# Row maxima as full-array products, and TensorE's step in another order, in a one-core transformer block

## The reference

```python
h = _L0_tok_ref(x, W, b, pos)                       # patches @ W.T + b + pos, 32 x 1024 x 64
q = h @ Wq.T + bq; k = h @ Wk.T + bk; v = h @ Wv.T + bv
scores = einsum('bid,bjd->bij', q, k) / 8           # 1024 x 1024 for each image
prob = softmax(scores)                              # rows with q[0] == 0 or k[0] == 0 become 0
h = layernorm(h + (prob @ v) @ Wo.T + bo)
idx = argmax(softmax(h @ gate_w + gate_b))          # expert of each token
pos = (cumsum(one_hot) * one_hot).sum(-1) - 1       # its place in the expert's list, kept if < C
y = relu(buf @ w1 + b1) @ w2 + b2                   # by expert, 64 -> 256 -> 64
h = layernorm(h + nan_to_num(y[idx, pos] * prb * kept))
```

## Time and profile before

| what | value |
|---|---|
| median of 3 runs | 1159.21 us (1153.78 to 1161.12) |
| profiled execution, span | 1163.1 us |
| TensorE busy | 1029.4 us, 89% |
| VectorE busy | 902.7 us, 78% |
| GpSimd busy | 692.6 us, 60% |
| ScalarE busy | 728.6 us, 63% |

### The profile page before, as it was taken

How to read it: one execution, slowest core, us unless ns; L and a number is a source line. 1 busy time by engine, 2 the same in 40 slices (tenths; PEclk the granted TensorE clock), 3 DMA queues, 4 the chain that set the end, 5 groups by cost and what they waited for, 6 DMA issues and landing times.

```text
span 1163.1 us, 18855 instructions
## 1 busy us (share of the span) xinstructions
PE 1029.4 (89%) x5534; PEld 582.2 (50%) x5534; DVE 902.7 (78%) x1847; ACT 728.6 (63%) x1142; POOL 692.6 (60%) x689
## 2 busy tenths in 40 slices
PE   4899999999999999999999999999999999736640
PEld 2455555555555555555555555555555555423320
DVE  5557787789898988889888988898988887654542
ACT  2255455667777777677777776776777667535540
POOL 0014445447676676667767666766666767765665
PEclk8699999999999999999999999999999999866775
DMA  5324335444444443535344443443453613034300
GB/s 129 93 69 106 96 89 141 111 104 111 115 122 115 109 121 96 148 87 150 95 125 120 114 104 106 124 119 101 106 137 79 154 37 92 20 96 121 98 18 10
DMA packets 76732, 118.93 MB, mean 102 GB/s; under 512 B 16652, under 2 KB 52959, under 8 KB 76630
## 3 DMA queue, kind: packets, MB, share of 16 engines
q1 hardware_dynamic: 59798, 100.61, 34.6%
q0 software_dynamic: 16832, 17.11, 4.6%
...
## 4 chain that ended last, share of the span: by engine, by line
PE 55%; DVE 24%; issue 10%; ACT 4%; SPq 2%; another core or an unknown queue 1%; POOL 1%; DMA 1%; POOLq 0%; DVEq 0%; ACTq 0%
PE p_u L575 15%; DVE mx L979 8%; PE p_st L559 8%; PE p_st L562 7%; PE p_sm L545 5%; PE p_misc L508 4%; PE p_misc L531 4%; PE p_misc L638 3%; PE p_misc L654 2%; PE p_misc L590 2%; ACT xh L754 2%; DVE ld L1045 1%; POOL out L1355 1%; DVE tt L1006 1%
## 5 line engine op out<-in xcount | busy, mean ns | idle before, releaser
L1343 POOL DMA_INDIRECT slots<-rows,idx x256 | 261.7, 1022 | 220.5 <-issue 151.4
L771 ACT ACTIVATE pT<-p_st 128x1024 f32<-128x1024 f32 x256 | 262.2, 1024 | 171.9 <-PE p_st L562 131.4
L979 DVE TENSOR_REDUCE mx<-p_sm 128x1 f32<-128x1024 f32 x252 | 307.3, 1220 | 80.1 <-PE p_sm L545 69.5
L1355 POOL DMA_INDIRECT out<-b_o,b_ix x270 | 286.9, 1063 | 111.9 <-issue 73.4
L575 PE MATMUL p_u<-pT,vv 128*64 128x512 f32 x1024 | 263.8, 615 | 0.0
L559 PE MATMUL p_st<-mQ,sK 128*128 128x512 f32 x512 | 184.2, 441 | 5.5 <-ACT pT L771 3.6
L562 PE MATMUL p_st<-mR,sR 72*128 72x512 f32 x512 | 161.8, 397 | 0.0
L545 PE MATMUL p_sm<-sK,mQ 64*128 64x512 f32 x252 | 130.7, 519 | 6.9 <-DVE mx L979 3.4
L559 PEld LDWEIGHTS p_st<-mQ,sK 128*128 128x128 f32 x512 | 79.7, 190 | 104.5 <-issue 81.3
L545 PE MATMUL p_sm<-hi,mQ 64*128 64x512 f32 x252 | 130.6, 518 | 0.0
L562 PEld LDWEIGHTS p_st<-mR,sR 72*128 72x128 f32 x512 | 97.4, 190 | 22.9
...
## 6 DMA issues: line engine op xcount, KB each, us to landing
...
```

The costliest lines, as they stand in the source:

```text
L771: act.activation(pT[k % 4][:, :], flat(p_st), ACT.Exp).then_inc(exp_done, 1)
L979: dve.tensor_reduce(mx[:, p, j:j + 1], flat(max_place(n, j)), AX.X, ALU.max).then_inc(max_done, 1)
L1343: pool.indirect_dma_start(slots, bass.IndirectOffsetOnAxis(ap=idx[:, p, j:j + 1], axis=0), rows[:, p, j, :], None, bounds_check=SLOTS - 1, ...
L1355: pool.indirect_dma_start(out_rows, bass.IndirectOffsetOnAxis(ap=b_ix[:, o, j:j + 1], axis=0), b_o[:, o, j, :], None, bounds_check=T - 1, ...
```

## The change

`max_scores` multiplies whole arrays: all 128 rows of mQ with all 128 rows of sK (high queries times high and low keys), for both halves of the keys. TensorE's step is written in another order, so that the first half of the weighted sum is not split, the first layer and the weighted sum stand together and the maxima behind them; `rows_turn` and `turn_back` come after the maximum and k = 3's projection; ScalarE no longer waits for maxima before it overwrites hi. On VectorE `row_max` comes first in each part, ahead of `attend` and `weigh`.

```diff
-                for a, keys in ((0, sK[t]), (1, hi[n % 2])):
-                    h = slice(a * D, (a + 1) * D)
-                    last = pe.matmul(max_place(n, j)[:, a, :], mQ[t][h, j * P:(j + 1) * P],
-                                     keys[h, a * HALF:(a + 1) * HALF], start=True, stop=True)
+                for a in range(2):
+                    last = pe.matmul(max_place(n, j)[:, a, :], mQ[t][:, j * P:(j + 1) * P],
+                                     sK[t][:, a * HALF:(a + 1) * HALF], start=True, stop=True)
                 last.then_inc(sm_done, 1)
...
+                m, back = chunk_of(b), chunk_of(b - 1)
                 for k in range(NT):
                     if has(0):
                         scores(b, par, c % 3, k)
...
                     if k == 2 and has(0):
-                        weighted_sum(b, par, 0, (0,))
-                    m, back = chunk_of(b), chunk_of(b - 1)
+                        weighted_sum(b, par, 0)
+                    if m is not None and k in (4, 5):
+                        up(m, k - 4)
+                    if k in (4, 5) and has(0):
+                        weighted_sum(b, par, 1, (k - 4,))
+                    if m is not None and k == 7:
+                        down(m)
+                    if has(1):
+                        if k == 6:
+                            project(b + 1, q, 1, has(2))
+                        max_scores(b + 1, (c + 1) % 3, third(1), k)
+                        if k == 3 and b >= 0:
+                            project(b + 1, q, 0, has(2))
                     if m is not None and k == 2:
                         rows_turn(m)
                     if back is not None and b <= NB and k == 2:
                         pe.wait_ge(t_ready, min(b, NB))
                         turn_back(back)
-                    if m is not None and k in (4, 5):
-                        up(m, k - 4)
-                    if m is not None and k == 7:
-                        down(m)
-                    if has(1):
-                        max_scores(b + 1, (c + 1) % 3, third(1), k)
-                        if k == 6 or k == 3 and b >= 0:
-                            project(b + 1, q, k // 6, has(2))
-                    if has(0):
-                        if k == 2:
-                            weighted_sum(b, par, 0, (1,))
-                        if k in (4, 5):
-                            weighted_sum(b, par, 1, (k - 4,))
-                        if k == 7:
-                            weighted_sum(b, par, 2)
+                    if k == 7 and has(0):
+                        weighted_sum(b, par, 2)
...
                     act.wait_ge(spread_r[p], of_parity(n - 2, p, 32))
-                    act.wait_ge(sm_done, NT * n - NT)
...
                 for j in range(NT):
-                    if j == 1 and inside and has(-1):
+                    if has(1):
+                        row_max(b + 1, q, j)
+                    if j == 1 and has(-1):
                         attend(b - 1, q)
                     if back is not None and j == 2:
                         weigh(back)
-                    if has(1):
-                        row_max(b + 1, q, j)
-                    if j == 1 and not inside and has(-1):
-                        attend(b - 1, q)
```

1 line of the change is left out of this document (removed).

## The result

The changed kernel takes 1189.18 us (median of 4 runs, 1186.25 to 1190.81) beside 1160.16 us for the kernel before on the same chip: 1.0248 times as long, 95% interval 1.0213 to 1.0282. Its profiled span is 1188.7 us, 25.6 more than before. It is slower, as forecast, by a little more than forecast (+22.9 in the span), and the time lies 1.2 us above the range. But the 25.6 us are made up differently from the sum of the prediction.

What follows compares the result with a forecast made beforehand. TensorE, VectorE and what stands behind VectorE were taken as near a tie. Even steps 11.6, odd 12.1, step 30 about 1.0, step 7 about 0.6, early -2.4 gave +22.9 us in the span, 1182 us; range 1155 to 1188.

Steps and rivals of the forecast that it cites:

- TensorE's sum, 0.0 per chunk step: TensorE in a chunk step: saved form switches pay for the doubled streaming and no more, 0.0 us.
- The rival that would have made the kernel faster: TensorE at k = 4 and 5: both places cost 0.04, not 0.24; 1147 us; chance 0.10.
- t_av held by the residual: VectorE, even steps: t_av issued while GpSimd's residual runs, held 1.2 us; VectorE loses about 1.0.
- the step hangs on vs through GpSimd: End of an even step: the squares' sum vs and GpSimd's ve slip by 1.0, making the step +1.05 us.
- idle 1 us at the step's start: TensorE, before the row-maximum transpose at each step's start: idle 1 us or more, as a sign the forecast is right.
- Even steps, +1.05: Eleven even steps (8 to 28): each 1.05 us longer, 11.6 together.
- Odd steps, +1.1: Eleven odd steps (9 to 29): each 1.1 us longer, 12.1 together.
- Both chains give +1.1: Odd steps: GpSimd's residual and scatters, and likewise VectorE's sixth maximum, come late enough to add 1.1 us.
- the prediction's second rival: Odd steps: the late completion vanishes, -0.25 us each, -2.8 for eleven; total about 1167; chance 0.15.
- Early steps, -2.4: The six steps without an expert chunk: together 2.6 us saved, taken as 2.4 since the first waits anyway.
- each saves 0.44: TensorE in each of the six steps without a chunk: 0.44 us less, together 2.6.
- The rival "absorbed": Steps' ends set by rows and ld absorb late maxima; only TensorE's sum is left, about 1157; chance 0.25.

Runs made afterwards that it cites:

- e12: The kernel before with a short GpSimd memset behind the second and fourth scatter of a row; 1131.57 us, ratio 1.0069.
- e17: The kernel before with VectorE's whole-unit step (t_f, t_av and what follows) behind the third maximum instead of the second; 1169.84 us, ratio 1.0034.
- e4: The changed kernel with VectorE's four unit instructions (t_f, t_av, t_cum, t_c) moved behind the third maximum and weigh; 1180.27 us, ratio 1.0167.
- e10: The kernel before with only VectorE's order of the changed kernel, TensorE's order and half-height products as before; 1150.05 us, ratio 1.0237.
- e13: The changed kernel itself, run again on another chip with its trace; 1203.11 us, ratio 1.0316.
- e14: The kernel before itself, run again in the same group as the changed kernel's rerun; 1168.78 us, ratio 1.0012.

## Why the prediction was right in sign, near in size, and wrong in its terms

It said 1182 within 1155 to 1188, and 1189.2 came. Three terms of the sum failed: the odd steps came out 16.6 us below theirs, the even ones 10.2 above and the early ones 7.2 above. That the total is off by so little is luck, and the even and early steps carried it over the top of the range.

**TensorE's sum, 0.0 per chunk step: right.** An odd step is 30.50 busy where e12's is 30.46. First layer and weighted sum take 1.07 (taken: 1.08), a full pair 0.47, or 0.57 to 0.58 at a change of form. The rival that would have made the kernel faster rested on 0.87 for the first layer alone; it falls.

**t_av held by the residual: right in place and length.** 1.32 against 0.17 is 1.15, and with the 0.24 that t_f no longer loses VectorE is 0.9 later, where the prediction said about 1.0. What it said of the end, that the step hangs on vs through GpSimd, agrees with the runs, though VectorE's own gapless end would look the same: ve comes 0.25, 0.95, 1.11 and 1.36 later in e17, e4, e10 and the changed kernel, and the step gets 0.25, 0.95, 1.09 and 1.55 longer. TensorE does not idle 1 us at the step's start, as was forecast, but 0.2 to 0.3 there and 0.87 ahead of the fourth pair.

**Even steps, +1.05: mis-sized, and not the hold's alone.** +1.5 is what undisturbed ones lose, eleven times 0.5 = 5 us more. The prediction put all of it on the hold. e4 takes the hold away and wins back 0.6 (0.85 in the disturbed steps); 0.95 stay. Two things were at nothing in the sum: the first maximum reaches VectorE 0.55 later, so that tt comes 1.6 later in the step and not 1.1, and without the hold VectorE would wait 0.61 for the third pair. No run takes the first of these away by itself. On top, five even steps have a late completion at 1.34 each, 6.7 us, where before one had, at 1.8.

**Odd steps, +1.1: the step that failed most.** "Both chains give +1.1" was added to steps of 31.7 as if the late completion in them were fixed and VectorE's slip came on top. Seven of the eleven odd steps are without it at that place, where before three were, and an undisturbed odd step takes 30.88, 0.1 to 0.3 more than an undisturbed one before. VectorE's order by itself does cost 0.9 there (e10, 31.5 beside e12's 30.6), but as TensorE's wait for tt at the transposes; in the changed kernel these stand behind the maximum and the whole weighted sum, so the wait is covered. The eleven steps came out at -4.5 and not +12.1: the prediction's second rival, half true, with the completions gone to the even steps, which it had not seen.

**Early steps, -2.4: wrong sign.** The steps 1 to 5 got 4.8 us longer. TensorE's own sum is -0.13 a step and not -0.44 (the prediction's own parts add up to -0.41), and 1.15 us of p_sm's turnaround come on top. The prediction had read the earlier trace rows for prices and never asked how far apart two maxima stand in the new order. The sentence "each saves 0.44" costed an order by its products alone.

**The range.** Its top, 1188, let even steps lose 1.2 at most and gave late completions no share but to vanish. In the span the terms missed by -16.6 (odd), +10.2 (even), +7.2 (early), +1.6 (step 30), +3.9 (behind the last image, +0.4 in e13 against e14) and -3.6 (start and step 0), together +2.7 with rounding. The -3.6 isn't shown to come from the change: 2.4 of it is step 0, which in TensorE's order of before took 28.12 us at a granted clock of 0.80 and 24.73 at 0.93 (e10). The rest of the distance from 1182 to 1189.2 lies outside the span: the span of before stood 3.9 us above the median that the prediction went by, that of after 0.5 below its own.

**The rival "absorbed"** had a right thing in view: ld's hold shrank from 1.53 to 0.75 and took up 0.8 of the slip in step 20. It was too little to save an even step.
